# Weight tiles turned as they are and signed from PSUM, and some work moved between the steps of a bi-WKV kernel

## The reference

```
x = x + ffn(wkv(r=x, k=side, v=side, w, u, cond), weight, bias)        # x, side: (4, 1024, 1024) f32

tf    = sigmoid(sum(cond))                                             # one number per batch
decay = exp(-exp(w)) * (0.5 + 0.5 * tf)                                # per batch and channel
ek = exp(min(k, 30));  ekv = ek * v
nf, df = forward scans  a = a * decay + (ekv, ek)    over T
nb, db = backward scans of the same
euk  = exp(min(u + k, 30))
num  = nf + nb - ekv + euk * v;  den = df + db - ek + euk
out  = sigmoid(r) * num / max(den, 1e-8) * (0.8 + 0.2 * tf)

alpha = mean(|weight|) per row;  bw = where(weight >= 0, 1, -1) * alpha
ffn(h) = h @ bw.T + bias
```

## Time and profile before

| | us |
|---|---|
| median of 3 runs (lowest, highest) | 512.13 (511.25, 512.55) |
| the profiled execution, own time | 513.52 |
| its span, first to last instruction | 511.5 |
| busy: PE / PEld | 352.3 (69%) / 206.7 (40%) |
| busy: DVE | 482.0 (94%) |
| busy: ACT | 413.9 (81%) |
| busy: POOL | 380.3 (74%) |

### The profile page before, as it was taken

One profiled execution on the slowest core, in us unless ns is written; L12 is line 12 of the kernel. 1 busy time (PEld: TensorE's weight loads), 2 busy tenths in 40 slices (PEclk: granted clock), 3 DMA queues, 4 the chain that ended last, 5 costly groups with the idle time before them and its releaser, 6 DMA issues.

```text
span 511.5 us, 5395 instructions
## 1 busy us (share of the span) xinstructions
PE 352.3 (69%) x1797; PEld 206.7 (40%) x1803; DVE 482.0 (94%) x346; ACT 413.9 (81%) x461; POOL 380.3 (74%) x210
## 2 busy tenths in 40 slices
PE   3323223332194877878597879869739999999996
PEld 2213223332152444335354445535425555544442
DVE  6999999999999699999999999999999999999566
ACT  3979899899979889988987989998797888894500
POOL 0067778748764987789788687889897799899483
PEclk9997666565678798898987989989987999999999
DMA  8878999999987498798979869989792679975379
GB/s 219 220 220 267 263 260 243 307 297 251 246 191 179 68 240 182 163 199 189 195 170 160 201 130 203 197 178 202 162 162 49 118 124 157 178 127 80 42 107 223
DMA packets 101283, 94.22 MB, mean 184 GB/s; under 512 B 2924, under 2 KB 93064, under 8 KB 100744
## 3 DMA queue, kind: packets, MB, share of 16 engines
q0 software_dynamic: 31440, 36.18, 46.9%
q1 hardware_dynamic: 67720, 56.65, 35.7%
q10 hardware_dynamic: 2096, 1.05, 0.8%
HBM read 60.31 MB, written 37.75 MB: 192 GB/s over the span
## 4 chain that ended last, share of the span: by engine, by line
POOL 27%; ACT 25%; PE 21%; issue 18%; DVE 7%; DMA 0%; SPq 0%; ACTq 0%; DVEq 0%; POOLq 0%
POOL wkv L379 11%; PE prod L447 8%; POOL acts L342 5%; POOL out_dram L355 4%; ACT x_nat L801 4%; POOL wkv L385 3%; ACT euk L659 3%; PE prod L488 3%; ACT terms L655 3%; ACT L806 3%; POOL terms L388 2%; ACT L801 2%; ACT rec L690 2%; PE sT L488 2%; PE kT L488 2%
## 5 line engine op out<-in xcount | busy, mean ns | idle before, releaser
L447 PE MATMUL prod<-acts,sgn 128*128 128x512 f16 x752 | 182.7, 399 | 0.0
L925 DVE TENSOR_TENSOR_SCAN terms<-cols,y_start,terms 128x1024 f32<-128x1024 f32 x64 | 147.0, 2337 | 1.1
L911 DVE TENSOR_TENSOR_SCAN terms<-cols,terms 128x1024 f32<-128x1024 f32 x64 | 142.8, 2272 | 0.0
L362 POOL TENSOR_TENSOR wkv<-wkv,terms 128x1024 f32<-128x1024 f32 x31 | 73.5, 2370 | 54.8 <-DVE wkv L954 54.8
L447 PEld LDWEIGHTS prod<-acts,sgn 128*128 128x128 f16 x752 | 77.2, 103 | 88.5 <-issue 16.7
L379 POOL TENSOR_TENSOR wkv<-euk,rec 128x1024 f32<-128x1024 f32 x31 | 82.1, 2648 | 33.2 <-ACT rec L692 33.1
L342 POOL TENSOR_TENSOR acts<-wkv,rec 128x1024 f16<-128x1024 f32 x30 | 78.4, 2612 | 5.0 <-ACT rec L701 4.9
L385 POOL TENSOR_TENSOR wkv<-wkv,rec 128x1024 f32<-128x1024 f32 x31 | 79.6, 2569 | 1.2 <-ACT wkv L753 1.2
L422 PE MATMUL prod<-ident,o_nat 128*128 128x128 f16 x64 | 8.3, 311 | 72.0 <-ACT o_nat L794 72.0
L422 PE MATMUL sT<-ident,x_nat 128*128 128x128 f32 x208 | 36.7, 334 | 27.5 <-ACT x_nat L801 11.2
L422 PE MATMUL kT<-ident,k_nat 128*128 128x128 f32 x248 | 43.4, 333 | 15.9 <-DVE own L942 15.8
(11 more groups left out here) (120 smaller groups left out, 585.7 us busy)
## 6 DMA issues: line engine op xcount, KB each, us to landing
terms<-own POOLq DMA_DIRECT2D x32, 512.0 KB, 5.2
out_dram<-in_x_dram SPq DMA_DIRECT2D x32, 512.0 KB, 7.2
k_nat<-in_fside_BxSxS_dram SPq DMA_DIRECT2D x30, 512.0 KB, 6.4
x_nat<-in_x_dram SPq DMA_DIRECT2D x26, 512.0 KB, 4.9
out_dram<-o_nat POOLq DMA_DIRECT2D x24, 512.0 KB, 8.4
y_fm<-in_L_ffn_weight_dram SPq DMA_DIRECT2D x8, 512.0 KB, 8.4
out_dram<-in_L_ffn_bias_dram POOLq DMA_DIRECT2D x8, 512.0 KB, 6.6
x_end<-in_x_dram SPq DMA_DIRECT2D x6, 512.0 KB, 8.7
```

The source lines that it names most:

```text
L362: pool.tensor_tensor(wkv[n % 2][:, :], wkv[n % 2][:, :], ekv[n % NV], ALU.mult).then_inc(st["base"], 1)
L447: ins = pe.matmul(made_in(u), view[:, c, m % CT * P:m % CT * P + P], acts[:, part, m // CT % 2 * CT + c, h * H:(h + 1) * H], start=(part = ...
L911: dve.tensor_tensor_scan(buf, d, buf, 0.0, ALU.mult, ALU.add).then_inc(st["F" + kind], 1)
L925: dve.tensor_tensor_scan(buf[:, ::-1], d, buf[:, ::-1], y_start[:, i:i + 1], ALU.mult, ALU.add)\
```

## The change

The weight tiles are turned by PE as they are loaded, in f32, into wT, which is now f32 and takes both banks of prod. ACT takes Sign straight from there into sgn. The copy with the scale SIGN, the f16 tiles s_nat and the f16 identity (with DVE's cast) are gone, and the three constants HI_SCALE, LO_GAIN and SIGN change so that the sign is 1.0. Abs and Sign of tiles 3 and 6 (`put_off`) come in ACT's next step, ahead of the exps.

The end sigmoids are taken two each in the sets of steps 3, 6 and 9; the set of step 8 and those in 12 are gone. SP loads the end tiles in steps 1 to 6, each with a semaphore of its own.

PE makes no unit in step 9, two in 10, three in 11, two in 12 and 13, three in 14, where it made two in each of 9 to 14. The derived `cleared` and `added` follow: one evacuation in step 10, three in 11, two in 12 and 13, three in 14 (before: one in step 9 and two in each of 10 to 14), and the stores of output tiles 0 to 12 come one step later each.

```diff
-HI_SCALE = 2.0 ** -4
-LO_GAIN = 2.0 ** 14
-SIGN = 0.5
+HI_SCALE = 2.0 ** -2
+LO_GAIN = 2.0 ** 7
+SIGN = 1.0
...
-    MORE = {19: 23, 20: 26, 21: 28, 22: 30, 23: 32, 24: 32, 25: 36, 26: 39, 27: 42, 28: 45}
+    MORE = {9: 0, 10: 2, 11: 5, 12: 7, 13: 9, 19: 23, 20: 26, 21: 28, 22: 30, 23: 32, 24: 32, 25: 36, 26: 39, 27: 42, 28: 45}
...
+    def put_off(n):
+        return 0 < n < CT and n % 3 == 0
...
-        wT = prod[:, 0, :].bitcast(F16).rearrange("p (c f) -> p c f", c=CT)
+        wT = prod[:, :, :].rearrange("p h (c f) -> p (h c) f", f=P)
...
# SP
-                    done(sp, "sgn", n - 2)
+                    done(sp, "wT", n - 2)
                     done(sp, "abs", n - 2)
...
-                if 2 <= n < 8:
-                    sp.dma_start(x_of(SOON + n - 2), tile_of(x, SOON + n - 2)).then_inc(s_soon, 16)
+                if 1 <= n < 7:
+                    sp.dma_start(x_of(SOON + n - 1), tile_of(x, SOON + n - 1)).then_inc(s_soon[n - 1], 16)
...
# PE
-                first = n % CT == 1 and n >= LAG
+                first = n % CT == 1 and n > LAG
...
-                    done(pe, "sgn", n)
-                    done(pe, "wTc", n - 1)
-                    turn(lambda c: wT[:, c, :], CT, lambda c: s_nat[p][:, c * P:(c + 1) * P],
-                         ident16[:, :]).then_inc(st["wT"], 1)
+                    landed(pe, w_in, n, p)
+                    done(pe, "sgn", n - 1)
+                    turn(lambda c: wT[:, c, :], CT, lambda c: w_nat[p][:, c * P:(c + 1) * P],
+                         ident[:, :]).then_inc(st["wT"], 1)
...
# ACT
+            def signs(n, p):
+
+                landed(act, w_in, n, p)
+                done(act, "abs", n - 1)
+                act.activation(junk, w_nat[p][:, :], ACT.Abs, accum_out=asum[:, n:n + 1])\
+                   .then_inc(st["abs"], 1)
+
+                done(act, "wT", n)
+                act.activation(sgn[:, :, n * P:(n + 1) * P], wT, ACT.Sign, scale=TINY_GAIN, bias=tiny[:, 0:1])\
+                   .then_inc(st["sgn"], 1)
...
-                if 1 <= n <= CT:
-
-                    done(act, "wT", n - 1)
-                    act.mul(sgn[:, :, (n - 1) * P:n * P], wT, SIGN).then_inc(st["wTc"], 1)
+                if put_off(n - 1):
+                    signs(n - 1, 1 - p)
...
-                if wt:
...
-                if n < SOON and (n % 3 == 0 or n == CT):
...
-                    for i in {CT: (0, 1, 2), CT + 1: (3, 4), CT + 4: (5,)}.get(n, ()):
-
-                        act.wait_ge(s_soon, 16 * (N - SOON))
+                if wt and not put_off(n):
+                    signs(n, p)
+                if n < SOON and n % 3 == 0:
...
+                    for i in range(2 * (n // 3 - 1), 2 * (n // 3)) if 3 <= n <= LAG else ():
+
+                        act.wait_ge(s_soon[i], 16)
                         act.activation(x_of(SOON + i), x_of(SOON + i), ACT.Sigmoid).then_inc(st["soon"], 1)
```

More of the change, by code:

```diff
@@ L123, in bi_wkv_binary_ffn @@
         park = [acts[:, 0, i, :].bitcast(F32) for i in range(CT)]
-        s_nat = [o_nat[p][:, 0:TT // 2, :].rearrange("p q f -> p (q f)").bitcast(F16) for p in range(2)]
         ident = sb("ident", [P, P])
-        ident16 = sb("ident16", [P, P], F16)
         rows = x_end[0:3 * CT, 0, 0:P]
@@ L178, in bi_wkv_binary_ffn @@
         b_in = [sem(f"b_in{q}") for q in range(TT)]
-        s_tail, s_plain, s_soon = sem("s_tail"), sem("s_plain"), sem("s_soon")
+        s_tail, s_plain = sem("s_tail"), sem("s_plain")
+        s_soon = [sem(f"s_soon{i}") for i in range(N - SOON)]
         st = {a: sem("d_" + a) for a in (
@@ L183, in bi_wkv_binary_ffn @@
             "ln", "rec", "chk", "two", "inv", "gate", "base", "hi", "hib", "lo",
-            "prod", "ev", "yT", "yc", "abs", "sgn", "wT", "wTc", "orow", "orow_sb", "early", "early_sb", "soon", "nat", "weighed", "joined", "scaled", "whole",
+            "prod", "ev", "yT", "yc", "abs", "sgn", "wT", "orow", "orow_sb", "early", "early_sb", "soon", "nat", "weighed", "joined", "scaled", "whole",
             "res", "prior_hi", "prior_hib", "prior_lo", "last_den", "last_ln", "last_rec", "last_chk", "last_inv", "last_gate",
@@ L581, in step @@
                 if wt:
-                    done(pe, "sgn", n)
-                    done(pe, "wTc", n - 1)
-                    turn(lambda c: wT[:, c, :], CT, lambda c: s_nat[p][:, c * P:(c + 1) * P],
-                         ident16[:, :]).then_inc(st["wT"], 1)
+                    landed(pe, w_in, n, p)
+                    done(pe, "sgn", n - 1)
+                    turn(lambda c: wT[:, c, :], CT, lambda c: w_nat[p][:, c * P:(c + 1) * P],
+                         ident[:, :]).then_inc(st["wT"], 1)
                 if not wt and not late:
-                    done(pe, "wTc", CT - 1)
+                    done(pe, "sgn", CT - 1)
                     pe.wait_ge(s_osc, 1)
@@ L637, in _ @@
         def _(act):
-            seed(act, "below", "expE", "expU", "sig", "ln", "rec", "two", "hi", "hib", "ev", "yc", "abs", "sgn", "wTc")
+            seed(act, "below", "expE", "expU", "sig", "ln", "rec", "two", "hi", "hib", "ev", "yc", "abs", "sgn")
             for i in range(NH):
@@ L706, in early_out @@
                 act.copy(park[i], park_bank[i]).then_inc(st["early_sb"], 1)
-            act.wait_ge(s_const, 4)
+            act.wait_ge(s_const, 3)
             act.wait_ge(s_ucol, 2)
@@ L785, in step @@
                         clear(sooner, later)
-                if wt:
-                    landed(act, w_in, n, p)
-                    done(act, "abs", n - 1)
-                    act.activation(junk, w_nat[p][:, :], ACT.Abs, accum_out=asum[:, n:n + 1])\
-                       .then_inc(st["abs"], 1)
-                    done(act, "wT", n - 2)
-                    act.activation(s_nat[p], w_nat[p][:, :], ACT.Sign, scale=TINY_GAIN, bias=tiny[:, 0:1])\
-                       .then_inc(st["sgn"], 1)
-                if n < SOON and (n % 3 == 0 or n == CT):
-                    if n % 3 == 0:
-                        for i in range(n, min(n + 3, SOON)):
-                            x_landed(act, i)
-                            act.activation(x_of(i), x_of(i), ACT.Sigmoid).then_inc(st["sig"], 1)
-                    for i in {CT: (0, 1, 2), CT + 1: (3, 4), CT + 4: (5,)}.get(n, ()):
-                        act.wait_ge(s_soon, 16 * (N - SOON))
+                if wt and not put_off(n):
+                    signs(n, p)
+                if n < SOON and n % 3 == 0:
+                    for i in range(n, min(n + 3, SOON)):
+                        x_landed(act, i)
+                        act.activation(x_of(i), x_of(i), ACT.Sigmoid).then_inc(st["sig"], 1)
+                    for i in range(2 * (n // 3 - 1), 2 * (n // 3)) if 3 <= n <= LAG else ():
+                        act.wait_ge(s_soon[i], 16)
                         act.activation(x_of(SOON + i), x_of(SOON + i), ACT.Sigmoid).then_inc(st["soon"], 1)
@@ L862, in per_batch @@
                 return col.unsqueeze(1).to_broadcast([P, B, CT])
-            dve.wait_ge(s_id, 2)
-            dve.tensor_copy(ident16[:, :], ident[:, :]).then_inc(s_const, 1)
             dve.memset(lnb[:, :], LN_BIAS).then_inc(s_const, 1)
```

## The result

The changed kernel takes 503.74 us, the median of four runs (503.15 to 503.94); beside it the kernel before took 512.34 (511.25 to 512.69). The ratio is 0.9834, 95% interval 0.9816 to 0.9851: 8.6 us, or 1.7%, faster. The forecast was 503.9. The profiled execution took 503.93, its span is 502.0; against the profiled execution of before (513.52) that is 9.6 us.

What follows compares the result with a forecast made beforehand. VectorE (DVE), busy 94% of the span, was taken as the bound. Gains 1.1 + 1.1 + 1.1 + 4.3 + 1.0 = 8.6, less 0.2 and 0.2, gave 8.2 us: from 512.13 to 503.9 us (503 to 504.9; wider range 502.2 to 506.8).

Steps and rivals of the forecast that it cites:

- The law: DVE's den waits for POOL's multiplies: a step loses chk's start after val less 4.6 to 4.8 us.
- Step 4: ACT's set in step 3 gets shorter, so ln comes earlier and step 4 loses 1.1 us instead of 2.2.
- Step 13: Step 12's set has one sigmoid less, so chk of step 13 comes earlier: gain 1.0 us.
- Steps 5 and 8: Exps may come late after the double weight tiles of steps 4 and 7: cost 0.1 us a step, bounds 0 and 0.7.
- Half of the sum, and it needs both.: Step 10 gains 4.3 us, needing step 8's backlog gone and no wait for PE in step 9.
- The third units: Third PE units in steps 11 and 14 delay ln of 13 and 16: 0.2 us in all, bounds 0 to 1.5 twice.
- the rule against: PE's bursts start cold after pauses: step 10's first unit is dearer by 2.6 us, the sum unchanged.
- rival 1: Low-clock first units in steps 11 and 14 delay ln of 13 and 16 by 1 to 1.5 us each; chance 0.13.
- 2 (overfilled steps): Double tiles overfill steps 4 and 7, so DVE waits for exps of 5 and 8: 0.4 to 1.4 us back; chance 0.12.
- 3: Slower: PE becomes the bound in steps 11 and 14, DVE waits up to 10 us twice: 524 us; chance 0.02.
- 4: ACT isn't freed: Sign on PSUM brings table loads or ACT waits for PE's turn: 508 to 510 us; chance 0.05.
- 5: More gain than counted: part of the 1.1 us in steps 4, 7, 10 clears: 501.5 to 502.5 us; chance 0.06.

Runs made afterwards that it cites:

- e1: Changed kernel, but with two units in each of steps 9 to 14 as before: 506.42 us.
- e3: Changed kernel, but with tiles 3 and 6 signed in their own steps, ahead of the set: 507.87 us.
- e7: Changed kernel, with the sets of steps 15, 18 and 21 made two sigmoids smaller, one larger and two larger: 507.03 us.
- e8: Changed kernel, with den in steps 16, 19 and 22 adding sT from PSUM instead of ek from SBUF: 501.23 us.
- e9: Changed kernel, with POOL doing inv before the low half in steps 4, 7, 10, 13, 16, and the next steps' store or bias DMA last: 500.1 us.
- e2: Changed kernel, but with end sigmoids as before, three in step 8, two in 9, one in 12: 504.01 us.
- e10: Kernel of e9 with step 22 also doing inv before the low half, the store of step 23 left in place: 499.51 us.
- e6: Kernel before, with only the new weight handling (raw tiles turned, Sign from PSUM, tiles 3 and 6 put off): 508.11 us.
- e4: Kernel before, with only the changed kernel's units (none in step 9, three in 11 and 14): 509.47 us.

## Why the prediction was right

**The law.** Chk's start after val, less 4.8, gives the losses of every kernel that has den and POOL's order as they were, but for steps 20 and 27: 5.97 gives 1.17 in step 4 (measured 1.17), 5.91 gives 1.11 in step 10 (1.13), 6.22 gives 1.42 in step 13 (1.42), 8.01 gives 3.21 (3.21), 8.25 gives 3.45 (3.46, first experiment, step 10). What the law rested on, that den and a running multiply of POOL exclude each other, was read from overlaps alone; the experiment with PSUM shows it. Two limits go with it. The formula as recorded (plus 7.0, minus 11.65, plus 0.1) gives 2.5 for step 4 and not 2.2: den ended 1.08 us behind inv, less than its own 1.23 and not 0.1 more. The 4.8 was the fit to that one row, and it is the constant that held. And the law wants POOL's three multiplies back to back. In steps 20 and 27 they are not: in the kernel before, chk of step 27 comes 4.42 us after val, under the 4.8, yet the low half behind it waits for ACT, and the step loses 1.34.

```profile
410.06 2.37 POOL L342 TENSOR_TENSOR acts<-wkv,rec 128x1024 f16<-128x1024 f32 x1 [1.66 <-ACT rec L701]
```

**Term by term.** Step 4: 1.1 foreseen, 1.05 measured. Step 7: 1.1, 1.08. Step 9: 1.1, 1.15. Step 10: 4.3, 4.32. Step 13: 1.0 less its share of the 0.2 for the third units, 0.66 measured. Steps 5 and 8 were charged 0.2 and lost nothing. The sum was 8.2; these steps give 8.26. That it is so close is in part luck: 0.2 was charged to steps 5 and 8 for nothing, and step 13 gave some 0.2 less than its term.

**Sign from PSUM** was taken at 1.1 between 1.00 and 1.15 and took 1.098. The raw turns cost PE 15.5 - 8.3 = 7.2 us in all (eight of four bytes 1.94, as in the earlier trace rows), 0.9 a step, taken as about 1; nothing waited for them. The turns of the signs in the kernel before, from its groups by line:

```profile
L422 PE MATMUL prod<-ident,o_nat 128*128 128x128 f16 x64 | 8.3, 311 | 72.0 <-ACT o_nat L794 72.0
```

**The room of the exps** was put at 0.3 us; they end 0.4 us before the vals of steps 5 and 8 want them.

**"Half of the sum, and it needs both."** The size was right, "needs both" too strong. The runs at step 10 make a square: 5.45 us lost before; 2.61 with the units alone out of step 9; 3.46 with all but that; 1.13 with all. So either part has a gain of its own, 2.84 and 1.99, and together they give 4.32. Of the rest it is the end sets that count there (alone 3.19), not the weights (alone 5.80).

**The third units, and the rule against.** The size, 0.2, looks about right: 0.27 by step 13 (1.42 against 1.15 in e1, which has none). But a third unit alone costs nothing: e3, e7 and e8 have the same three units in step 11 and lose 1.18, 1.17 and 1.17 in step 13. What sets the profiled execution of the changed kernel apart is the first unit of step 11, 5.43 us, against 4.41, 4.14 and 4.74 in those three; e9, where it takes 5.46, has chk of step 13 late too (6.25 us after val). So it takes three units and a dear first one. Against rival 1 I had argued that it could not be dear there, since in step 11 the burst of step 10 has just ended; that was wrong. The timelines of PE and of ACT in the changed kernel:

```profile
153.66 7.88 PE L449 MATMUL prod<-acts,sgn 128*128 128x512 f16 x32
...
168.70 5.43 PE L449 MATMUL prod<-acts,sgn 128*128 128x512 f16 x16
...
178.29 3.62 PE L449 MATMUL prod<-acts,sgn 128*128 128x512 f16 x16
```

```profile
178.12 0.78 ACT L671 ACTIVATE y_fm<-prod,bcol,oscale 128x512 f32<-128x512 f32 x1 [2.64 <-PE prod L449]
```

The two units of step 10 took 7.88 us together, 0.6 more than two of 3.62, though PE had done only turns in step 9; the first unit of step 11 took 5.43. The windows of the changed kernel (us, busy of each engine, granted PE clock, DMA share) show it:

```profile
149.00:154.00 5.00, 4.02 (x17) 3.43 (x18) 5.00 (x5) 4.97 (x5) 3.18 (x2) 0.50 0.41 103
153.70:155.20 1.50, 1.50 (x5) 0.57 (x4) 1.50 (x2) 1.47 (x3) 0.00 (x0) 0.50 1.05 243
155.60:161.50 5.90, 5.90 (x28) 2.50 (x26) 5.72 (x5) 5.34 (x6) 5.90 (x3) 1.00 0.92 245
...
168.70:172.20 3.50, 3.50 (x10) 1.29 (x9) 3.36 (x4) 3.23 (x4) 3.50 (x3) 0.50 0.85 278
172.60:174.00 1.40, 1.40 (x9) 0.67 (x7) 1.40 (x2) 1.07 (x2) 1.37 (x1) 1.00 0.01 0
```

The clock is at 0.50, the lower of its two levels of 1.2 and 2.4 GHz, while PE turns (149 to 154). Both bursts start there: the one of step 10 stays at it for about 1.6 us and is 0.6 dearer, the one of step 11 for about 3.6 us and is 1.8 dearer. So the dear unit came one step later than I had it, ACT waited 2.64 us for the second product, and chk of step 13 came at 6.22 instead of 5.96. It was rival 1 in small: its marks, "den over 2.5 in 13" and "a wait of ACT for prod over 2 us", did appear, at 0.27 us instead of 1 to 1.5, and only in one of the two places: step 16 lost 1.13 as foreseen. The second mark is a poor one: in e8 ACT waited 2.61 us for the same product, and step 13 lost 1.17. The Trainium skill (TensorE: Matmul & The Clock Gate, "HAM oscillation") says that after the pauses between bursts every burst starts cold. Both bursts above do; the price was 0.6 and 1.8 us, where the prediction had the rule put 2.6 on step 10. It doesn't hold of every burst here: in e2 and e10 the clock is back at 1.00 in the last turns ahead of step 11's first unit (in e2 from 167.6, the unit starting at 167.85), and that unit takes 3.62. What decides when the clock comes back no run here shows.

**What the sum did not have.** Step 27 lost 1.34 before and nothing after. In PE's timeline the first unit of step 26 took 4.82 us before and takes 3.61 after:

```profile
386.40 4.82 PE L447 MATMUL prod<-acts,sgn 128*128 128x512 f16 x16
```

```profile
377.94 3.61 PE L449 MATMUL prod<-acts,sgn 128*128 128x512 f16 x16
```

The change touches nothing there. Among kernels equal in those steps 20 loses 0.46 to 1.63 and 27 0 to 1.35, so I don't count this as a gain of the change: 8.26 + 1.34 are the 9.6 us of the profiled pair, where the medians are 8.6 apart. Step 27's loss goes with that unit in all twelve traces: the unit takes 3.61 us in the four where the step loses 0.03 or less, and 3.75, 3.82, 3.98, 4.11, 4.33, 4.71, 4.80 and 4.82 where it loses 0.31, 0.35, 0.53, 0.67, 0.85, 1.25, 1.35 and 1.34. Whether a kernel has its dear unit in every execution, one trace of each can't tell.

**Which edit brings it.** I priced the end sigmoids' move by its gains in steps 9, 13 and part of 10, and its cost in steps 4 and 7 inside the sum of ACT's work there, so that one can't see what it is worth: by the table 1.17 + 1.12 = 2.3 us lost in 4 and 7 against 0.20 + 1.47 + 0.69 = 2.4 won in 9, 10 and 13. The account is even, by the medians too (504.01 and 503.74; in the kernel before, ratio 1.0005). The gain is that of the weights with tiles 3 and 6 put off (e6: 2.22 + 2.20 + 0.93 - 0.35 = 5.0 us by steps) and of step 9 without units (e4: 2.84), with 0.4 more at step 10 where e6's wait for PE is gone: 8.2 of the 8.3. The second experiment, which has these two and the old end sets, shows it in one kernel: 13.1 us lost in steps 4 to 13 before, 4.9 there.

**The rivals.** 2 (overfilled steps) fell in the changed kernel with 0.4 us to spare and came true in the ninth experiment, 0.78 us, as soon as DVE was faster. 3 and 4 fell: no step with PE as the bound, and 19 table loads. 5 was not seen.
